# The first graph layer in rounds of two heads by 1564 destinations

## What is computed

```python
h = (x @ W).reshape(N, heads, D)
es = jnp.sum(h * a_src, axis=-1)
ed = jnp.sum(h * a_dst, axis=-1)
e = jax.nn.leaky_relu(es[src] + ed[dst], NEG_SLOPE)
emax = jax.lax.stop_gradient(jax.ops.segment_max(e, dst, num_segments=N))
ex = jnp.exp(e - emax[dst])
denom = jax.ops.segment_sum(ex, dst, num_segments=N)
alpha = ex / denom[dst]
out = jax.ops.segment_sum(h[src] * alpha[:, :, None], dst, num_segments=N)
x1 = jax.nn.elu(out.reshape(N, heads * D) + b)
```

## Time and profile before

| | us |
|---|---|
| median of three runs (3573.38 to 3575.60) | 3573.63 |
| span of the profiled execution | 3578.1 |
| front, steps and counts, up to the first row block | 626 |
| the changed stage, first STT to last sum | 640.2 to 1418.4 |
| its end, up to the last tile of the next projection | 1444 |
| second graph layer, experts, attention, tail | 1444 to 3578 |

### The profile page before, as it was taken

The page is one execution under the profiler, slowest core; times in us unless marked ns, Lnnn a source line. Parts: engine busy times, 40 slices in busy tenths (PEclk is TensorE's granted clock), DMA queues, the critical chain, the costliest instruction groups (busy, mean ns, idle before and its releaser), DMA issues. The chain is left out here.

```text
span 3578.1 us, 46445 instructions
## 1 busy us (share of the span) xinstructions
PE 3011.8 (84%) x16281; PEld 1597.0 (45%) x16282; DVE 2777.0 (78%) x3285; ACT 2210.7 (62%) x3171; POOL 340.6 (10%) x476
## 2 busy tenths in 40 slices
PE   3226777888888888899769889999999999979998
PEld 2212333333333333688669753333333333357775
DVE  8887998899999998454432369999999999944333
ACT  3100378899999998011123268898888888924432
POOL 0000000011111111000035300110111101100000
PEclk9557999999999999999879989999999999989998
DMA  2000245344444343443166553333333333310000
GB/s 57 0 0 12 81 166 200 103 114 120 116 116 115 108 115 92 169 160 137 53 197 212 184 178 98 88 91 86 86 90 87 90 86 90 85 64 23 8 8 14
DMA packets 208306, 348.78 MB, mean 97 GB/s; under 512 B 38337, under 2 KB 142255, under 8 KB 208106
## 3 DMA queue, kind: packets, MB, share of 16 engines
q1 hardware_dynamic: 192330, 317.88, 29.4%
q0 software_dynamic: 15776, 28.26, 2.6%
HBM read 277.62 MB, written 61.88 MB: 95 GB/s over the span
## 5 line engine op out<-in xcount | busy, mean ns | idle before, releaser
L935 PE MATMUL acc<-weights_then_messages,messages 128*64 128x400 f32 x3200 | 609.0, 514 | 93.3 <-DVE weights_then_messages L1009 65.8
L2035 PE MATMUL acc<-weights,keys_and_values 128*64 128x400 f32 x3200 | 633.3, 517 | 2.9 <-DVE weights L2194 1.5
L2194 DVE SCALAR_TENSOR_TENSOR weights<-x,counts 128x1600 f32<-128x1600 f32 x304 | 555.0, 1826 | 18.4 <-ACT x L2161 7.9
L935 PEld LDWEIGHTS acc<-weights_then_messages,messages 128*64 128x64 f32 x3200 | 206.8, 137 | 492.0 <-issue 207.7
L1009 DVE SCALAR_TENSOR_TENSOR weights_then_messages<-rho,kappa,counts 128x800 f32<-128x800 f32 x400 | 414.7, 1080 | 4.8 <-PE acc L935 4.4
L2158 ACT ACTIVATE x<-scores 128x800 f32<-128x800 f32 x496 | 409.0, 852 | 13.7 <-PE scores L2022 13.6
L2022 PE MATMUL scores<-q,keys_and_values 32*128 32x400 f32 x3200 | 387.0, 553 | 32.9 <-ACT x L2156 32.1
L957 ACT ACTIVATE weights_then_messages<-rho,wx 128x800 f32<-128x800 f32 x400 | 362.0, 954 | 26.0 <-DVE weights_then_messages L1014 16.9
L2035 PEld LDWEIGHTS acc<-weights,keys_and_values 128*64 128x64 f32 x3200 | 195.3, 137 | 390.9 <-issue 345.9
L1014 DVE TENSOR_TENSOR weights_then_messages<-weights_then_messages,counts 128x1600 f32<-128x1600 f32 x200 | 364.6, 1823 | 5.6 <-ACT weights_then_messages L962 5.6
L962 ACT ACTIVATE weights_then_messages<-weights_then_messages,kappa 128x800 f32<-128x800 f32 x400 | 360.7, 950 | 0.0
(11 more groups left out here) (371 smaller groups left out, 3564.0 us busy)
## 6 DMA issues: line engine op xcount, KB each, us to landing
counts<-edge_counts SPq DMA_DIRECT2D x200, 400.0 KB, 3.2
counts<-edge_counts SPq DMA_DIRECT2D x400, 200.0 KB, 2.4
edge_counts<-counts_out SPq DMA_DIRECT2D x40, 1000.0 KB, 4.2
counts<-edge_counts SPq DMA_DIRECT2D x24, 1600.0 KB, 7.0
w_first<-in_L_ffn_W_dram SPq DMA_DIRECT2D x57, 512.0 KB, 3.6
w_second<-in_L_ffn_W_dram SPq DMA_DIRECT2D x8, 512.0 KB, 7.8
y<-sums POOLq DMA_DIRECT2D x32, 100.0 KB, 2.6
denominators<-sums_of_weights POOLq DMA_DIRECT2D x32, 100.0 KB, 3.8
```

The costliest lines, as they stand in the source:

```text
L935: ins = nc.tensor.matmul(acc[64 * o:64 * o + 64, p, h, 0:CH], msg[:, t, r % 2 * Q + q, :], w[:, T % WR, q, half(h)], start=(t == 0), stop= ...
L2035: ins = nc.tensor.matmul(acc[64 * e:64 * e + 64, p, 0:CH], msg[:, t, r % KF * 2 + p, D * e:D * e + 2 * D], w[:, U % WR, 2 * p + e, :], sta ...
L2194: ins = nc.vector.scalar_tensor_tensor(out=w[:, U % WR, :, :], in0=out, scalar=EXP_HI, in1=counts, op0=ALU.min, op1=ALU.mult)
```

## The change

- Shape of a round. `Q` is 2 heads, a round covers `PARTS` x `CP` = 4 x 391 = 1564 destinations; there are 2 ranges of destinations and 4 groups of heads, 8 rounds as before. 3128 columns are worked on in place of 3200.
- A step has one STT of 1564 columns for head 0, one relu and one addition on ACT for head 1 (the addition waits for the relu just before it), and one TT of 1564. PE waits once, for the TT, and then does its 8 matmuls of 391 columns. The STT of a step waits until PE has used all of step T-2, `w` is still a ring of 2.
- A row block is two of the four parts of a head; steps 8, 10, 12, 14 and 10, 12, 14, 16 stay. The sums are copied at step 1, in two halves as before.
- The counts of a step are 128 x 1564; each count is loaded in four rounds, not in two.
- Messages are packed with 33 columns to a head. PE still reads 64 columns, of which the last 31 belong to the next head and give sums that nobody reads; `beyond` is 31 columns of zeros behind the last head.
- Numerators of two rounds are stacked in `y` (4 heads by 32 features by 1564 destinations). Division and ELU are done once for two rounds, during rounds 2, 4 and 6 and after the last. Pool's last instruction also waits until all row blocks of that range of destinations are made.
- At the end 12 tiles of the projection are early; the last ELU is done in two pieces, of 868 and 696 columns.

```diff
@@ stage_front
+                nc.gpsimd.memset(g.beyond, 0.0)
...
-                    link(nc.vector.tensor_copy(g.msg[:, :, two, D:D + R], av[:, :, two].unsqueeze(3).to_broadcast([P, NT, 2, R])))
+                    link(nc.vector.tensor_copy(g.msg[:, :, two, D], av[:, :, two]))
@@ stage_gat_aggregate
-    Q = 4
-    CW = 2 * CH
-    ROUNDS = NP // CW * (H // Q)
+    Q, PARTS, CP = 2, 4, 391
+    CW = PARTS * CP
+    HALVES, GROUPS = 2, H // Q
+    ROUNDS = HALVES * GROUPS
     CR, WR = 4, 2
     ROW_AT, RHO_AT, BOUND_AT = (8, 10, 12, 14), (10, 12, 14, 16), 22
-    SUMS_AT, INVERT_AT, DIVIDE_AT, ELU_AT = 0, 6, 11, 13
-    SPREAD = CW * Q // P
-    EARLY, ELU_AFTER, SLOTS = (NP - CW) // P, 12, 4
-    msg, kap, bias, wdb = g.msg, g.kap, g.bias, g.wdb
+    SUMS_AT, INVERT_AT, DIVIDE_AT, ELU_AT = 1, 6, 11, 13
+    SPREAD_OVER = 92
+    SPREAD = CW * Q // SPREAD_OVER
+    EARLY, ELU_AFTER, SLOTS = CW // P, 10, 4
+    kap, bias, wdb = g.kap, g.bias, g.wdb
...
-        mx = g2.place[:, WR * Q * CW:WR * (Q + 2) * CW].rearrange("p (r q c) -> p r q c", q=2, c=CW)
-        sums = core.sb(ctx, "sums", [P, 2, CW])
+        mx = g2.place[:, WR * Q * CW:WR * (Q + 1) * CW].rearrange("p (r c) -> p r c", c=CW)
+        sums = core.sb(ctx, "sums", [P, PARTS, CP])
         den = core.sb(ctx, "denominators", [P, CW])
-        spread = core.sb(ctx, "denominators_spread", [P, SPREAD])
+        spread = core.sb(ctx, "denominators_spread", [SPREAD_OVER, SPREAD])
...
-        acc = core.ps(ctx, "acc", [P, 2, 2, 512])
+        acc = core.ps(ctx, "acc", [P, PARTS, 512])
...
-        W_T, MX_T, USED_T = 3, 2, 2
+        W_T, USED_T = 2, 2
...
+        def head(r, q):
+            return r % GROUPS * Q + q
 
         def columns(r):
-            return r // 2 * CW
-
-        def make_row(r, q):
-
+            return r // GROUPS * CW
...
+        def message(t, j):
+
+            first = (t * H + j) * g.step
+            return g.flat[:, first:first + 64]
...
-                o = 64 * (q % 2) + D
-                pool.dma_start(den_dram[0, r, q:q + 1, :], sums[o:o + 1, q // 2, :]).then_inc(s_raw, 16)
-            if r:
-                pool.wait_ge(s_y, r)
+                o = 64 * q + D
+                pool.dma_start(den_dram[0, r, q:q + 1, :], sums[o:o + 1, :, :].rearrange("p m n -> p (m n)")).then_inc(s_raw, 16)
+            if r >= 2 and r % 2 == 0:
+                pool.wait_ge(s_y, r // 2)
             for q in range(Q):
-                o = 64 * (q % 2)
-                pool.dma_start(y[D * q:D * q + D, :], sums[o:o + D, q // 2, :]).then_inc(s_stack, 16)
+                pool.dma_start(y[home(r, q):home(r, q) + D, :], sums[64 * q:64 * q + D, :, :].rearrange("p m n -> p (m n)")
+                               ).then_inc(s_stack, 16)
             pool.wait_ge(s_raw, (r + 1) * Q * 16)
...
+            group = r // 2
             if m == 0:
-                act.wait_ge(s_div, r + 1)
-                ins = nc.scalar.activation(y[:, :], y[:, :], ACT.Identity, bias=bcol[:, r % 2:r % 2 + 1])
+                act.wait_ge(s_div, group + 1)
+                ins = nc.scalar.activation(y[:, :], y[:, :], ACT.Identity, bias=bcol[:, feature_half(r):feature_half(r) + 1])
...
-                pe.wait_ge(s_y, ROUNDS - 2)
-                pe.wait_ge(s_exp, ROUNDS * Q)
+                pe.wait_ge(s_y, 2)
+                pe.wait_ge(s_exp, ROUNDS * PARTS)
             if t == EARLY:
-                pe.wait_ge(s_y, ROUNDS - 1)
+                pe.wait_ge(s_y, 3)
                 pe.wait_ge(s_last, 2)
+            if t == (CW + LAST_CUT) // P:
+                pe.wait_ge(s_last, 4)
...
+        LAST_CUT = 19 * P - CW
+        last_k = feature_half(ROUNDS - 1)
+
+            dve.wait_ge(s_div, GROUPS)
+            for i in range(2):
+                part = last_piece(i)
+                nc.vector.tensor_scalar(y[:, part], y[:, part], bcol[:, last_k:last_k + 1], None, ALU.add).then_inc(s_biased, 1)
+            for i in range(2):
+                part = last_piece(i)
+                out = XT[:, last_k, columns(ROUNDS - 1) + part.start:columns(ROUNDS - 1) + part.stop]
+                dve.wait_ge(s_biased, i + 1)
+                nc.vector.tensor_scalar(out, y[:, part], 0.0, None, ALU.max).then_inc(s_last, 1)
+                dve.wait_ge(s_last, 2 * i + 1)
+                dve.wait_ge(s_elu, 3 * (GROUPS - 1) + 2 * i + 2)
+                nc.vector.scalar_tensor_tensor(out=out, in0=ey[:, part], scalar=-1.0, in1=out, op0=ALU.add, op1=ALU.add).then_inc(s_last, 1)
+
+        def last_exp(act, i):
+
+            part = last_piece(i)
+            before = 3 * (GROUPS - 1) + 2 * i
+            act.wait_ge(s_biased, i + 1)
+            nc.scalar.activation(ey[:, part], y[:, part], ACT.Relu, scale=-1.0).then_inc(s_elu, 1)
+            act.wait_ge(s_elu, before + 1)
+            nc.scalar.activation(ey[:, part], ey[:, part], ACT.Exp, scale=-1.0).then_inc(s_elu, 1)
...
-                        for p in range(2):
+                            m = ROW_AT.index(t)
+
+                            pe.wait_ge(s_exp, (r + 1) * PARTS + m - 1)
+                            make_row(r + 1, m)
+                        pe.wait_ge(s_w, (T + 1) * W_T)
+                        for half in range(2):
                             if t == 0 and r:
 
-                                pe.wait_ge(s_free, 2 * (r - 1) + p + 1)
-                            pe.wait_ge(s_w, T * W_T + 2 + p)
-                            for h in range(2):
-                                for o in range(2):
-                                    q = 2 * p + o
-                                    ins = nc.tensor.matmul(acc[64 * o:64 * o + 64, p, h, 0:CH], msg[:, t, r % 2 * Q + q, :],
-                                                           w[:, T % WR, q, half(h)], start=(t == 0), stop=(t == NT - 1))
+                                pe.wait_ge(s_free, 2 * (r - 1) + half + 1)
+                            for m in (2 * half, 2 * half + 1):
+                                for q in range(Q):
+                                    ins = nc.tensor.matmul(acc[64 * q:64 * q + 64, m, 0:CP], message(t, head(r, q)),
+                                                           w[:, T % WR, q, m * CP:(m + 1) * CP], start=(t == 0), stop=(t == NT - 1))
                             ins.then_inc(s_used, 1)
...
-                        for e in range(2):
-                            j = r % 2 * Q + 2 + e
-                            nc.scalar.activation(mx[:, T % WR, e, :], rho[:, r % 2, 2 + e, :], ACT.Relu, bias=nkap[:, t, j:j + 1]
-                                                 ).then_inc(s_relu, 1)
-                        for e in range(2):
-                            j = r % 2 * Q + 2 + e
-                            act.wait_ge(s_relu, T * MX_T + e + 1)
-                            nc.scalar.activation(mx[:, T % WR, e, :], mx[:, T % WR, e, :], ACT.Identity, bias=kap[:, t, j:j + 1]
-                                                 ).then_inc(s_mx, 1)
+                        nc.scalar.activation(mx[:, T % WR, :], rho[:, r % 2, 1, :], ACT.Relu, bias=nkap[:, t, j:j + 1]).then_inc(s_relu, 1)
+                        act.wait_ge(s_relu, T + 1)
+                        nc.scalar.activation(mx[:, T % WR, :], mx[:, T % WR, :], ACT.Identity, bias=kap[:, t, j:j + 1]).then_inc(s_mx, 1)
                         if r and t == SUMS_AT:
                             copy_sums(act, r - 1)
                         if t in RHO_AT and r + 1 < ROUNDS:
-                            q = RHO_AT.index(t)
+                            m = RHO_AT.index(t)
 
                             act.wait_ge(s_w, r * NT * W_T)
-                            act.wait_ge(s_row, (r + 1) * Q + q + 1)
-                            make_rho(r + 1, q)
-                        if r and 0 <= t - ELU_AT < 3:
+                            act.wait_ge(s_row, (r + 1) * PARTS + m + 1)
+                            make_rho(r + 1, m)
+                        if r and r % 2 == 0 and 0 <= t - ELU_AT < 3:
...
+                    if r % 2 == 0 or r == ROUNDS - 1:
+                        continue
+
+                    group = r // 2
+                    first = columns(r)
+                    pool.wait_ge(s_elu, 3 * group + 2)
                     nc.gpsimd.tensor_scalar(y[:, :], y[:, :], 0.0, -1.0, ALU.max, ALU.add).then_inc(s_upper, 1)
-                    pool.wait_ge(s_upper, r + 1)
-                    pool.wait_ge(s_elu, 3 * r + 3)
-                    nc.gpsimd.tensor_tensor(XT[:, r % 2, columns(r):columns(r) + CW], y[:, :], ey[:, :], ALU.add).then_inc(s_y, 1)
-                pool.wait_ge(s_y, ROUNDS - 1)
+                    pool.wait_ge(s_upper, group + 1)
+                    pool.wait_ge(s_elu, 3 * group + 3)
+
+                    pool.wait_ge(s_row, min((r // GROUPS + 1) * GROUPS, ROUNDS) * PARTS)
...
-                        for q in range(2):
-                            j = r % 2 * Q + q
-                            if q == 0 and T >= WR:
```

(20 more changed lines are left out.)

## The result

The kernel before takes 3573.6 us and the changed one 3585.4 us, medians of twelve runs each; the ratio is 1.0027, with a 95% interval from 1.0018 to 1.0035. The forecast was 3562.0 us, in a range from 3546 to 3580.

A forecast was written before the change was run, and what follows sets the result against it. DVE was taken as the bound, PE as slower around row blocks. Stage -16.7, tail +5.8 and front -0.7 gave -11.6 us, a span of 3566.5; medians lie 4.5 below, so 3562.0 us, range 3546 to 3580.

The forecast's parts named there:

- Rivals C: STT on DVE: its overhead grows with its length, leaving less to stall on; 16 us more, 3578 us; chance 5%.
- Rival D: Count loads come late, each engine needing 213 GB/s; at 12 us a load 0.5 us a step, 3660 us; chance 5%.
- front and start: Ahead of the rounds: shorter factor copies save 0.4 us and four first row blocks 0.3 us, 0.7 us less.
- The row window: Steps around PE's four row blocks: DVE waits for PE and loses 5.8 us in every round that makes rows.
- rival E: Row blocks slip into PE's gaps and the window costs 1 us: 33 us less, 3530 us; chance 8%.
- rival B: PE gains nothing from 391 columns or its clock is lower in the window: window 7 us, 3568 us; chance 15%.
- clamp 1.70: Clamp of rho, in the sums of rounds 0 to 6: counted as 1.70 us of DVE time a round.
- first step 1.55: Start of round 0: the TT waits for two dependent activations, 3.3 us instead of 1.76, adding 1.55 us.
- copies of the sums: ACT's copies, moved to step 1: PE gets its bank later and the STT two steps on loses 0.2 us.
- Times 1564/800: Pool's ELU beside DVE: earlier STT losses scaled by columns give 3.4 to 4.4 us a group; 3.6 taken.
- Rival A: Pool's ELU holds DVE off for its whole instructions: 12.6 us a group, 3589 us; chance 7%.
- The tail: End of the stage: 13 late projection tiles instead of 7 and a longer division, 5.8 us longer in all.

The follow-up runs named there:

- e2: The changed kernel with the clamp of rho cut into four pieces of 782 columns behind steps 19 to 22: 3577.4 us against 3576.0 for the kernel before.
- e1: The changed kernel with Pool's two ELU instructions cut to one column each, every wait kept: 3562.5 us against 3576.0 for the kernel before.
- e7: The changed kernel with Pool's two ELU instructions moved to DVE, behind steps 15 and 16 of rounds 2, 4 and 6: 3567.4 us against 3574.5 before.
- e3: The changed kernel with w a ring of three steps, three count slots and the maxima in their own tile: 3547.3 us against 3576.0 before.
- e4: The kernel before with only the coarser waits: PE waits for a whole step, the first STT for all of step T-2: 3615.0 us against 3576.0.
- e12: The changed kernel with the half-step release given back, PE taking head 0's eight passes first, then head 1's: 3593.9 us against 3572.3 before.

## Why the prediction was wrong

**Durations, ACT, loads: right.** STT 1.84, TT 1.78, 3.46 us a step, an activation 1.60, the pair 3.13, a load 4.4 us with no wait for it, as forecast. Rivals C and D are out: an overhead growing with the length would give 1.96 us an STT, and the DMA share of 0.69 made nobody late (forecast 0.75). Rival D's 213 GB/s are what the sixteen DMA engines bring together, not each: 219 and 204 in the two rounds shown. The 0.7 us of front and start can't be told, since the stage's beginning scatters over 6 us between traces.

**The row window: right.** Forecast 5.8 us a round, measured 1.73 + 1.25 + 1.24 + 1.25 = 5.5 in odd rounds. The way of summing PE's and DVE's work between two points held to 0.3 us, so rival E (the window costs 1 us) is out, and B with it: its 7 us do not appear, though the lower clock it names does, at another place. In even rounds the division takes the place of stalls, as said.

**The clamp: wrong.** The term "clamp 1.70" failed. It counts the clamp as DVE's own work and puts the wait behind it at nothing; I had not asked what PE does meanwhile. It has nothing for 2.30 us, its clock falls, and its next passes take twice as long just where a whole step must be done before the STT. Measured is a wait of 1.28 us at step 0 of each of the rounds 1 to 7. In round 0, where PE had idled 7.91 us before its first step, step 2 waits 1.25 us, behind "first step 1.55", which had only the TT's wait for ACT (1.41). These are 10.2 us that the sum did not have. The 1.4 us that it had for the copies of the sums did not appear, since the wait ahead of them covers them: **8.8 us** net. Their 0.2 us a round were right in themselves (0.16 where the clock stays up). e2 took the gap away, and the waits behind the clamps went with it.

The kernel before shows the same slow passes in three of its seven rounds, and no STT waits for PE there. The TT's wait for ACT is 0.82, 0.75 and 0.75 us in just these rounds (2, 4 and 6) and 0.42 in the others, so only about half of the 0.82 us that the prediction puts down to ACT's two copies is theirs; the rest goes with the clock.

**Pool: wrong.** "Times 1564/800" of 0.59 and the low end of 1.15 to 1.67 us gave 3.6 us a group; measured are 7.16, three times 3.6 more, **10.7 us**. Two things failed. The 0.59 us did not scale: a tensor_scalar costs a TT 0.83 ns a column up to 1024 and is 2.6 us dearer at 1300 and 1564, and 800 columns gave no sign of that. And the low end of the second range was no cheap pass. That STT had waited 0.41 us for PE while Pool was already at work, so part of Pool's time fell in the wait; the row with 1.67 us, the only one of the seven passes without such a wait, was the price, and 1.67 x 1.955 = 3.27 is what was measured (3.24). "Six of the seven passes are there" was an argument about a place, when the place is what changed.

Rival A, with 7%, had the mechanism in part: it priced 12.6 us a group, and the group costs 7.2. Its point of decision was set at 10 us, yet 7.2 were enough together with the clock. The Trainium skill says (SBUF — State Buffer, SBUF: two separate sides) that a VectorE instruction with two SBUF inputs, as the STT and the TT are, and a GpSimd instruction that reads SBUF lock each other out for a whole instruction. The traces agree for GpSimd's tensor_tensor (3.24 us lost of 3.54) and do not for its tensor_scalar, which costs 0.65 us of its 3.36 at 782 columns.

**The tail: right in kind.** 32.3 us from the start of the early tiles to the next stage's first instruction, before 25.6 (1418.4 to 1444.0): 6.7 us more against 5.8. The late tiles begin sooner than forecast (18.4 us after the last sum, not 19.0), but the clock is low there too: PE has idled 7.69 us, the granted clock is 0.53 from 1436.2 to 1440, and the 13 tiles take 13.27 us where 0.87 us a tile makes 11.3.

Of the stage's forecast 761.5 us, 8.8 + 10.7 bring 781.0; measured are 781.9 (635.93 to 1417.84), before 778.2. The steps did give 41 us. The row windows took back 7 x 5.5 = 38 of them (in even rounds the division's 1.70 us is a part of the 5.5), and what was to be a margin of 11 fell to the clock and to Pool. Two side figures of the prediction do not follow from its own terms: the windows take back 7 x 5.8 = 40.6 us and not "some 29", and rival B's window of 7 us costs 7 x 1.2 = 8.4 us and not 6; neither enters the forecast. Two causes are shown by runs: Pool by e1 and e7, the clock after the clamp by e2 and by e1's two rounds without it. That the coarser release is what makes DVE wait at all is shown by e3 and e4; e12 shows only half of it, since its passes are slower. Not shown is what makes the jump between 1024 and 1300 columns, what decides whether the clock falls after a given gap, and where some 5 us of e4's loss lie.

## What to carry to other kernels

Longer instructions on the bounding engine save their overhead, but with the same two buffers they also make the wait for the reader coarser: sum the work of both engines between two waits, and if the reader is nearly as busy, give the gain its third buffer first. Where an engine does a single long thing at a seam (a clamp here), look at what the others have to do meanwhile; an idle TensorE can come back at half rate and hand the stall back. A cost that one engine causes on another is measured at the length at which it will run, on a row without another wait in it.

## What was not expected of the hardware

- After 2.1 to 2.3 us without work TensorE's passes can come back at half rate (16 passes in 4.54 us, 32 in 7.18). After the gap behind a clamp they did so in seven rounds of seven in after, five of seven with Pool's ELU left out, three of seven with a third buffer and three of seven before. After the gaps of 1.08 us beside the pieces of the clamp they never did (16 passes in 2.85 us).
- GpSimd's (Pool's) tensor_scalar slows DVE's TT by 0.83 ns a column up to 1024 columns (0.32, 0.43, 0.65 and 0.84 us at 391, 540, 782 and 1024; an STT by 0.07 us less) and by 3.70 and 3.92 us at 1300 and 1564. Its tensor_tensor does so by 2.1 ns a column at 391, 782 and 1564.
- Eight passes in a row of one 64-column tile cost TensorE 0.4 us more than eight with two tiles by turns (3.4 against 2.7 us for sixteen).
